# GpSimd's order of work in the state-space stage of a two-layer kernel: scatters behind the agings, tables read in place, last taps ahead of the second growth

## The reference

```python
proj = xn @ W_in.T + b_in                     # gate 2048, hBC 2304, dt 32
hBC  = silu(sum(xp[:, j:j+S] * conv_w[:, j] for j in range(4)))   # 4 taps along the tokens
h, Bm, Cm = hBC                               # 32 heads of 64; state size 128
# in chunks of tokens, A_cum the running sum of A*dt in a chunk:
Y_diag = (Cm Bm^T * exp(A_cum_l - A_cum_s), lower triangle) @ (h * dt)
Y_off  = Cm @ state * exp(A_cum)
state  = state * exp(A_cum_last) + Bm^T @ (h * dt * exp(A_cum_last - A_cum))
y = (Y_diag + Y_off + D*h) * silu(gate)
out = rmsnorm(y) @ W_out.T
```

## Time and profile before

| | |
|---|---|
| median of 3 runs | 2253.31 us (2252.2 to 2258.63) |
| the profiled execution's own time | 2269.01 us |
| its span in the trace | 2267.2 us |
| the state-space stage in it | from 149 us to about 1390 us |
| busy over the whole span | PE 93%, DVE 74%, POOL 61%, ACT 56% |
| clock granted to PE, mean over the span | 0.986 of full |

### The profile page before, as it was taken

The page is one execution under the profiler, slowest core; times in us unless marked ns, Lnnn a source line. Parts: engine busy times, 40 slices in busy tenths (PEclk is TensorE's granted clock), DMA queues, the critical chain, the costliest instruction groups (busy, mean ns, idle before and its releaser), DMA issues. The chain is left out here.

```text
span 2267.2 us, 43809 instructions
## 1 busy us (share of the span) xinstructions
PE 2108.1 (93%) x13681; PEld 1690.3 (75%) x13681; DVE 1669.2 (74%) x3408; ACT 1269.3 (56%) x2755; POOL 1375.4 (61%) x1248
## 2 busy tenths in 40 slices
PE   4879999999999999999999998999989989999997
PEld 2447777777777777777777776877744679999997
DVE  5779888899989999999999995667766853333332
ACT  2457777777777777777777773222235653333332
POOL 1326776676767777767777775777764524444443
PEclk9989999999999999999999999999999999999999
DMA  8854555555555555555645554886564065232221
GB/s 319 333 148 123 149 139 147 136 141 140 143 139 138 146 142 155 140 135 144 156 137 145 145 136 128 246 276 219 155 244 138 1 221 137 47 49 48 46 46 24
DMA packets 193458, 328.83 MB, mean 145 GB/s; under 512 B 49043, under 2 KB 135188, under 8 KB 192980
## 3 DMA queue, kind: packets, MB, share of 16 engines
q1 hardware_dynamic: 135972, 227.40, 35.9%
q0 software_dynamic: 26640, 53.38, 8.9%
q10 hardware_dynamic: 30624, 45.25, 6.5%
HBM read 240.19 MB, written 86.53 MB: 144 GB/s over the span
## 5 line engine op out<-in xcount | busy, mean ns | idle before, releaser
L1058 DVE SCALAR_TENSOR_TENSOR m_cv<-m_hp,conv,m_cv 128x256 f32<-128x256 f32 x864 | 415.0, 482 | 42.4 <-ACT m_cv L952 15.5
L875 POOL TENSOR_TENSOR m_er<-m_er,m_cT 128x1024 f32<-128x1024 f32 x128 | 307.0, 2399 | 91.3 <-DMA m_er<-eacum_rows_dram 64.6
L990 ACT ACTIVATE m_ar<-m_ar,m_ta 128x128 f32<-128x128 f32 x1024 | 312.6, 390 | 0.8
L1149 PE MATMUL m_hp<-xnT,wpj 128*128 128x259 f32 x1152 | 305.3, 388 | 7.6 <-PEq L145 4.5
L1157 PE MATMUL m_gp<-xnT,wpj 128*128 128x256 f32 x1024 | 270.7, 386 | 0.8 <-ACT m_gT L970 0.6
L1586 PE MATMUL e_u<-e_xgT,xnT 128*128 128x128 f32 x2272 | 266.8, 276 | 1.0 <-ACT xnT L1524 1.0
L1208 PE MATMUL m_out<-wo,m_gT 128*128 128x256 f32 x1024 | 257.5, 385 | 10.8 <-DVE m_gT L1097 10.7
L1149 PEld LDWEIGHTS m_hp<-xnT,wpj 128*128 128x128 f32 x1152 | 213.2, 192 | 70.8 <-issue 34.7
L1586 PEld LDWEIGHTS e_u<-e_xgT,xnT 128*128 128x128 f32 x2272 | 260.8, 193 | 1.3 <-ACT xnT L1524 1.2
L882 POOL TENSOR_TENSOR m_hdd<-m_hdt,m_tb 128x512 f32<-128x512 f32 x128 | 133.7, 1044 | 186.8 <-DVE m_hdt L1073 186.8
L1503 POOL DMA_INDIRECT out<-e_y,target x71 | 112.2, 1581 | 204.5 <-ACT e_y L1535 97.2
(11 more groups left out here) (338 smaller groups left out, 4273.2 us busy)
## 6 DMA issues: line engine op xcount, KB each, us to landing
m_ar<-acum_rows_dram SPq DMA_DIRECT2D x512, 128.0 KB
m_er<-eacum_rows_dram SPq DMA_DIRECT2D x128, 512.0 KB, 4.2
rows_by_slot<-blank_rows ACTq DMA_DIRECT2D x1, 18576.0 KB, 81.7
e_xg<-rows_by_slot ACTq DMA_DIRECT2D x131, 129.0 KB
m_xrow<-xn_rows SPq DMA_DIRECT2D x32, 512.0 KB, 7.1
arena<-y_rows SPq DMA_DIRECT2D x16, 1024.0 KB, 7.2
arena<-in_w SPq DMA_DIRECT2D x5, 1024.0 KB
wpj<-in_w_proj SPq DMA_DIRECT2D x1, 4352.0 KB, 23.9
```

Of the source, the lines that this page charges most:

```text
L875: g.tensor_tensor(er[:, t], er[:, t], middle(cT[:, t * P:(t + 1) * P], HQ), ALU.mult).then_inc(scaled.sem, 1)
L990: ins = a(row, row, ACT.Exp, bias=ta[:, kept(i, t), q * HQ + h:q * HQ + h + 1])
L1058: v_.scalar_tensor_tensor(o, hp[n % 2][:, j:j + BLK], conv[:, c, j:j + 1], o, ALU.mult, ALU.add).then_inc(tapped.sem, 1)
L1149: ins = mm(hp[n % 2][:, 0:PW], w_proj[:, kd, col:col + P], xpad[:, kd, ds(i * BLK, PW)], start=kd == 0, stop=kd == KD - 1)
```

## The change

Three edits, all in `ssd_phase`:

1. The tables `ta` and `tb` and their events are gone. ACT's exponentials and POOL's `weigh` and `age` read the table `tabs` itself, which is written before the stage. The two copies on DVE and the waits around them go.
2. POOL's order in a slot: `scale(b)`, `weigh(a)`, `add_squares(last)`, `weigh(b)`, `age(a)`, `age(b)`, `fold_squares(.., 0)` if due, then the two scatters, then `scale(u, 1)` and the rest. So the scatters go from the head of the slot to behind the agings, and `weigh(a)` goes ahead of `add_squares(last)`, which waits for ACT's square of a gated result.
3. DVE does `taps(late[1])` ahead of `grow(b)` instead of behind it.

```diff
@@ ssd_phase
-        ta = sb("ta", [P, TB + 1, H])
-        tb = sb("tb", [P, TB + 1, 2, H])
-        ta_done, tb_done, c_copied = ev("sums_copied", 1), ev("decays_copied", 1), ev("c_copied", 1)
+        c_copied = ev("c_copied", 1)
@@ gpsimd: weigh, age
-                    tb_done.wait(pool, i, 1)
-                                    bcast(tb[:, kept(i, t), 0, q * HQ:(q + 1) * HQ], HP), ALU.mult).then_inc(hddd.sem, 1)
+                                    bcast(tabs[:, i * TB + t, 1, q * HQ:(q + 1) * HQ], HP), ALU.mult).then_inc(hddd.sem, 1)
-                    g.tensor_tensor(sv, sv, bcast(tb[:, kept(i, t), 1, q * HQ:(q + 1) * HQ], HP), ALU.mult).then_inc(aged.sem, 1)
+                    g.tensor_tensor(sv, sv, bcast(tabs[:, i * TB + t, 2, q * HQ:(q + 1) * HQ], HP), ALU.mult).then_inc(aged.sem, 1)
@@ gpsimd: body
                 def body(n, w, u):
+                    a, b, last = older(n - 1), newer(n - 1), newer(n - 2)
+                    if b:
+                        scale(*b)
+                    if a:
+                        weigh(*a)
+                    if last:
+                        add_squares(*last)
+                    if b:
+                        weigh(*b)
+                    if a:
+                        age(*a)
+                    if b:
+                        age(*b)
+                    if last and last[1] == NQ - 1:
+                        fold_squares(last[0], 0)
                     if w:
                         i, q = w
                         for m in range(q * TB, q * TB + TB):
...
-                    a, b, last = older(n - 1), newer(n - 1), newer(n - 2)
-                    if b:
-                        scale(*b)
-                    if last:
-                        add_squares(*last)
-                    if a:
-                        weigh(*a)
-                    if b:
-                        weigh(*b)
-                    if a:
-                        age(*a)
-                    if b:
-                        age(*b)
-                    if last and last[1] == NQ - 1:
-                        fold_squares(last[0], 0)
                     if u:
                         scale(*u, 1)
@@ scalar: exps
-                        ta_done.wait(act, i, 1)
-                        ins = a(row, row, ACT.Exp, bias=ta[:, kept(i, t), q * HQ + h:q * HQ + h + 1])
+                        ins = a(row, row, ACT.Exp, bias=tabs[:, i * TB + t, 0, q * HQ + h:q * HQ + h + 1])
@@ vector: body
-                    if w and w[1] == 0:
-                        i = w[0]
-                        exped.wait(dve, i, -1)
-                        v_.tensor_copy(ta[:, both(i)], tabs[:, ds(i * TB, TB), 0, :]).then_inc(ta_done.sem, 1)
...
-                        hddd.wait(dve, i, -1)
-                        aged.wait(dve, i, -1)
-                        v_.tensor_copy(tb[:, both(i)], tabs[:, ds(i * TB, TB), 1:3, :]).then_inc(tb_done.sem, 1)
...
                     if b:
                         finish(*b)
-                        grow(*b)
                     if w:
                         taps(w[0], late[1])
+                    if b:
+                        grow(*b)
```

## The result

The changed kernel takes 2301.8 us (median of 4 runs, 2297.13 to 2307.84) against 2254.69 us for the kernel before: a ratio of 1.0209, 95% interval 1.0176 to 1.0242. It is slower by 47 us where 10 us less were forecast; the forecast range ended at 2263 us. Run once more among the experiments, beside the kernel before on that chip, it gave 1.0228 (1.0194 to 1.0262).

A forecast was written before the change was run, and what follows sets the result against it. PE was taken to set the pace, DVE close behind. Taps -4.5 us and the q3-to-q0 passage -5.0 us sum to -9.5 us: profiled 2269.0 becomes 2259.5, median 2244 us; range 2234 to 2263 us.

The forecast's parts named there:

- What bounds the kernel, and where PE waits: Middle of the stage: PE sets the pace; it waits 19.2 us behind ACT's silu and 19.7 us for DVE.
- Tables in place, 0.1 to 0.2 us a block: Dropping DVE's two table copies a block wins 0.1 to 0.2 us where DVE is late at gm, nothing elsewhere.
- `weigh(a)`, worth nothing alone: At the mixes: keep and weigh(b) come up to 0.8 us earlier, but the lead is gone by the slot's end.
- It leads by 0.09 us: q2 slot: b's gating product starts at 905.12, scale(u, 1) at 905.21, so the product goes first and takes 0.69 us.
- The second rival: In q2 slots scale(u, 1) beats b's gating product and delays the taps: +5 to +13 us; chance 0.25.
- The q3 slot, `gm` 0.65 us later and PE's wait 1.33 us: b's product waits behind scale(u, 1) until 926.27, so PE's wait for gm grows from 0.68 to about 1.33 us.
- The passage: From the q3 slot to the q0 slot: DVE-caused waits of 26.3 us in 16 blocks become 21.3, net -5.0 us.
- Taps ahead of growth, -0.28 us a block: q3 slot's head: earlier last taps free ACT's silu and the fourth projection; -4.5 us over 16 blocks.
- No queue gains a wait: Moved scatters delay no load: token rows came over half a slot before, SP's next load awaits older scatters.

The follow-up runs named there:

- e11: e1 with weigh(a) back behind add_squares(last); ratio 0.9849 to the kernel before.
- e4: Changed kernel with a POOL wait for b's gating product behind scale(u, 1), ahead of add_squares(a); 2273.18 us, ratio 1.0014 to the kernel before.
- e9: Kernel before with only the last taps put ahead of the second growth; ratio 0.9992.
- e10: e1 with taps and growth back in their old order; ratio 0.9926 to the kernel before.
- e1: Changed kernel with a POOL wait for b's gating product between the scatters and scale(u, 1); 2233.11 us, ratio 0.9834 to the kernel before.
- e6: Kernel before with only a POOL wait for b's gating product ahead of scale(u, 1); 2317.62 us, ratio 1.0224.

## Why the prediction was wrong, step by step

- **What bounds the kernel, and where PE waits.** Held. The ACT chain stayed (20.4 us against 19.2), and all that moved sits in the heads of the q3 and q0 slots. (The 0.87 us between two projections is the usual distance in the trace of before, but does not stand in the earlier trace rows.)
- **Tables in place, 0.1 to 0.2 us a block.** Not resolved: 0.9993 (0.9969 to 1.0017) fits both 2 us and nothing.
- **`weigh(a)`, worth nothing alone.** Held: mixes 2.35 instead of 3.14 us, slots unchanged (e11).
- **"It leads by 0.09 us", and so b's product "takes 0.69 us and ends at 905.81".** This is the step that failed. The times were right, the lead even 0.15 us. Wrong was that the first to start wins. It was taken from instructions of POOL that had been waiting for a transfer, whose recorded start comes when their wait ends. Behind a scatter, a `scale` whose waits are met wins although it is recorded to start later (105 of 111). The product took 4.28 us, and the q2 slots, from which -4.5 us were forecast, lost 30.1 us. The sentence of the Trainium skill in "SBUF — State Buffer", section "SBUF: two separate sides", that whichever starts first has the ports, agrees with the trace at 696.42 (0.02 us were enough) and not at 532.53 (0.15 us were not), unless "starts" is read as the meeting of its waits.
- **The second rival named the right mechanism and the wrong price**, +5 to +13 us where it is +47. It let the product go when `scale` ends, 0.55 us being read from a `scale` that stood behind a wait for its rows. Behind a scatter DVE is kept out of the next instruction too, 1.2 us more in q2 and q3 slots (e4). With `add_squares(a)` held back, which is what the rival priced, the loss is 3 us (e4, 1.0014). Nor did it count the slots that go on as in the 7.69 us case. The trace of before had shown it, in a q1 slot right behind the second scatter, POOL and then DVE, and the prediction did not read it:

```profile
876.20 2.38 POOL L875 TENSOR_TENSOR m_er<-m_er,m_cT 128x1024 f32<-128x1024 f32 x1
878.53 1.05 POOL L882 TENSOR_TENSOR m_hdd<-m_hdt,m_tb 128x512 f32<-128x512 f32 x1
```
```profile
877.99 3.82 DVE L1065 SCALAR_TENSOR_TENSOR m_ar<-m_ar,m_gm 128x1024 f32<-128x1024 f32 x2
```

  The mixes, ready at 877.99, were not let in at 878.53 but at about 879.6, 1.5 us over their 2.35.
- **The q3 slot, `gm` 0.65 us later and PE's wait 1.33 us.** Its mechanism, a product held up by `scale`, was right; the term was mis-sized by `add_squares(a)` again: 2.14 us of waiting and work foreseen, 3.42 measured, and 2.59 us of PE's time where 1.33 were foreseen. The passage was to gain 5.0 us; the q3 slots lost 11.0.
- **Taps ahead of growth, -0.28 us a block.** Right in place and near in size for the q2 slot (0.37 us, e9 and e10). That it also fills the wait for `update(b)` in the q3 slot, 0.67 us, was missed; it shows only where nothing else holds DVE up.
- **No queue gains a wait.** Held: PE never waits for `er` rows, and in e1, with the scatters in the new place, no wait but ACT's is left.

## What to carry to other kernels

When GpSimd work is moved, list not only what it now meets but what stands behind it with its waits already met. Behind a scatter, here, a DVE instruction with both inputs in SBUF waited until GpSimd had a gap; elsewhere only until the current instruction ended. A price read in one of the two places does not hold in the other. A small wait that GpSimd can afford, on the very instruction that must not be held up, can decide what the reordering is worth (here 0.9834 against 1.0209), but only where the queue behind it has room: the same wait on the kernel before cost 2.2%. A margin of a tenth of a microsecond in a sum is a coin toss between two prices, and the worse price deserves to be worked out as fully as the forecast.

## What the runs showed of the hardware beyond what was expected

- GpSimd instructions that follow a scatter and each other without a gap keep DVE out across all of them: 2.35 + 1.26 + 2.33 + 1.03 us, one DVE product of 7.69 us. With a wait between the first two it was let in after the first (3.05 us). In a string that did not begin behind a scatter it was let in after the current one (349 of 350 boundaries, against 3 of 274).
- A DVE copy with one input, both sides in SBUF, is held up by GpSimd as well: the copy of `tb`, 0.22 us alone and 1.12 in e6.
- The end of a scatter does not hold up a gating product: 0.69 us with a scatter running beside its start (509.65 in e1), while a scatter that begins as such a product runs takes 1.27 instead of 1.00 us.
- After some of PE's waits its clock falls for a few us. In the changed kernel PE waits 2.60 us until 793.1, and from 794 to 797 us the granted clock is 0.50, 1.2 instead of 2.4 GHz; that slot lasts 22.78 instead of 21.10 us. After a wait of the same length that ends at 716.9 the clock stays at 1.00. In e6 a wait of 2.19 us comes 14 times; 8 of them are followed by such a stretch, and those q3 slots last 22.8 instead of 21.1 us. What tells the two kinds of wait apart is not shown.

```profile
794.00:797.00 3.00, 3.00 (x10) 2.34 (x9) 1.63 (x6) 0.56 (x1) 2.63 (x2) 0.50 0.19 36
717.00:720.00 3.00, 3.00 (x17) 2.56 (x17) 2.12 (x6) 1.04 (x2) 1.90 (x1) 1.00 0.16 26
```

The best version found is e1, the changed kernel with one wait of GpSimd for b's gating product. What bounds it now is PE's own work: PE is busy for 291.41 of 300 us from 700 to 1000 us. The only waits left are those behind ACT, 27.2 us in 900.
